# Diagonal matrices and FFN products moved from GpSimd to VectorE, and two more PSUM banks for a feed-forward stage

## The reference: what is computed

```python
xn = layernorm(x)                                   # over the features, eps 1e-5
# recurrent branch, D_INNER = 2048, 16 states per channel
x1, x2 = split(xn @ in_proj_w.T + in_proj_b)        # 2048 + 2048 features
u = silu(causal_conv4(x1) + conv_b)                 # depthwise, 4 taps
h[t] = dA * h[t-1] + dB * u[t];  y[t] = sum_n C[:, n] * h[t][:, n]
s = (y * silu(x2)) @ out_proj_w.T + out_proj_b
# feed-forward branch, HIDDEN = 3072, int weights / 127
g = silu((silu(xn @ wg.T) * (xn @ wu.T)) @ wd.T)
out = x + s * g
```

## Time and profile before

| | |
|---|---|
| median of 3 runs | 4397.6 us (4396.36 to 4398.45) |
| profiled execution, its own time | 4412.73 us |
| its span, slowest core (core 0) | 4411.2 us; the 8 cores 4382.3 to 4411.2 |
| PE busy | 2854.1 us (65%), mean granted clock 0.80 |
| DVE busy | 2549.1 us (58%), of which the 512 scans 2352.0 |
| POOL busy | 2634.7 us (60%), of which the 512 diagonals 1771.2 |
| ACT busy | 774.2 us (18%) |

### The profile page before, as it was taken

One profiled execution on the slowest core, in us unless ns is written; L12 is line 12 of the kernel. 1 busy time (PEld: TensorE's weight loads), 2 busy tenths in 40 slices (PEclk: granted clock), 3 DMA queues, 4 the chain that ended last, 5 costly groups with the idle time before them and its releaser, 6 DMA issues.

```text
span 4411.2 us, 32972 instructions; the slowest of 8 cores (4382.3 to 4411.2 us)
## 1 busy us (share of the span) xinstructions
PE 2854.1 (65%) x10752; PEld 1123.5 (25%) x10752; DVE 2549.1 (58%) x771; ACT 774.2 (18%) x1159; POOL 2634.7 (60%) x1060
## 2 busy tenths in 40 slices
PE   3666666666666567788636666666666665687976
PEld 1222222222222123233312222222222221233333
DVE  2888788887888811000138878888788888010001
ACT  6111111111111111231161111111111110112311
POOL 0788887888788820231008878888788888102310
PEclk9777777777777779899957777777777776897889
DMA  3010111101111053633320000110101000526333
GB/s 93 17 19 17 19 22 24 19 17 19 27 20 19 12 122 62 154 63 68 79 84 19 17 19 17 29 19 17 19 17 29 17 19 15 134 48 158 60 65 77
DMA packets 84542, 195.57 MB, mean 44 GB/s; under 512 B 10272, under 2 KB 27040, under 8 KB 84384
## 3 DMA queue, kind: packets, MB, share of 16 engines
q0 software_dynamic: 46080, 109.07, 15.1%
q1 hardware_dynamic: 38304, 84.40, 5.7%
HBM read 268.93 MB, written 33.55 MB: 69 GB/s over the span
## 4 chain that ended last, share of the span: by engine, by line
PE 37%; POOL 26%; issue 25%; DMA 6%; ACT 3%; DVE 2%; SPq 1%; POOLq 0%; DVEq 0%; ACTq 0%
POOL bfb L588 19%; PE ps_y L600 5%; POOL bfb L529 5%; PE ps_a L437 5%; PE ps_a L796 4%; PE ps_b L437 4%; PE ps_b L796 4%; PE ps_a L486 3%; PE ps_b L486 2%; PE ps_b L546 2%; PE ps_b L699 2%; PE ps_a L699 2%; POOL bfa L396 2%; PE ps_a L546 2%; DMA bfa<-wur 2%
## 5 line engine op out<-in xcount | busy, mean ns | idle before, releaser
L580 DVE TENSOR_TENSOR_SCAN bfb<-aa,bfb 128x2048 bf16<-128x2048 f32 x512 | 2352.0, 4654 | 451.5 <-PE ps_y L600 404.6
L588 POOL TENSOR_SCALAR bfb<-idbs,cbt 128x128 bf16<-128x128 bf16 x512 | 1771.2, 3468 | 307.7 <-PE ps_y L600 305.1
L600 PE MATMUL ps_y<-bfb 128*128 128x512 bf16 x2048 | 706.7, 488 | 920.9 <-POOL bfb L588 881.7
L739 DVE TENSOR_TENSOR bfb<-f32a,s_sb 128x1024 bf16<-128x1024 f32 x32 | 39.2, 1226 | 1108.8 <-ACT f32a L805 1108.8
L600 PEld LDWEIGHTS ps_y<-bfb 128*128 128x128 bf16 x2048 | 207.9, 112 | 1346.3 <-issue 1249.4
L437 PE MATMUL ps_a<-xnt,bfa 128*128 128x512 bf16 x1536 | 453.0, 448 | 85.8 <-DMA bfa<-wur 31.7
L529 POOL TENSOR_SCALAR bfb<-idbs,convws 128x128 bf16<-128x128 bf16 x128 | 310.6, 2440 | 176.4 <-DVE bfb L516 176.4
L396 POOL TENSOR_TENSOR bfa<-s_sb 128x1024 bf16<-128x1024 bf16 x96 | 381.5, 3974 | 11.8 <-ACT s_sb L450 11.1
L437 PE MATMUL ps_b<-xnt,bfa 128*128 128x512 bf16 x1536 | 385.9, 397 | 0.0
L486 PE MATMUL ps_a<-xnt,bfa 128*128 128x512 bf16 x1024 | 343.0, 495 | 4.2 <-ACT xnt L363 2.7
L450 ACT ACTIVATE s_sb<-ps_a,cnss 128x512 bf16<-128x512 f32 x192 | 131.9, 687 | 895.6 <-PE ps_a L437 894.2
(11 more groups left out here) (54 smaller groups left out, 1534.1 us busy)
## 6 DMA issues: line engine op xcount, KB each, us to landing
f32a<-x SPq DMA_DIRECT2D x64, 512.0 KB, 7.1
bfa<-wgr POOLq DMA_DIRECT2D x96, 256.0 KB, 3.7
bfa<-wur POOLq DMA_DIRECT2D x96, 256.0 KB, 3.6
bfb<-wdr POOLq DMA_DIRECT2D x32, 768.0 KB, 6.7
bfa<-winr POOLq DMA_DIRECT2D x64, 256.0 KB, 4.3
xg_spill<-bfb SPq DMA_DIRECT2D x32, 512.0 KB, 2.6
bfa<-woutr POOLq DMA_DIRECT2D x32, 512.0 KB, 5.2
bfb<-xg_spill SPq DMA_DIRECT2D x128, 128.0 KB, 5.2
```

Of the source, the lines that this page charges most:

```text
L580: (lambda i, n, hs, uslot: lambda e: e.tensor_tensor_scan(hs, sb["aa"][:, 16 * i + n:16 * i + n + 1].broadcast_to([128, T]), uslot, 0.0, A ...
L588: (lambda i, n, dg: lambda e: e.tensor_scalar_mul(dg, sb["idbs"][:], sb["cbt"][:, 16 * i + n:16 * i + n + 1]))(i, n, dg),
L600: (lambda n, pc, dg, hs: lambda e: e.matmul(ps["y"][:, 512 * pc:512 * (pc + 1)], dg, hs[:, 512 * pc:512 * (pc + 1)], start=(n == 0), stop= ...
```

## The change

Three kinds of work go from POOL's list to DVE's, at the same places of the order: the 128 tap diagonals of the convolution (L529), the 512 state diagonals `dg` (L588) and the 96 products `hm` (L396). They raise `sv` in place of `sg`, and who waited for `sg` waits for `sv`; `sg` goes. Diagonal n no longer waits for the matmuls of n-2 by itself: it stands right behind scan n in DVE's list, and that scan waits for them. The matmuls of n wait only for diagonal n, which comes after scan n. POOL is left with the weight loads.

The second part touches the stage of 48 feed-forward units at cb = 1: it gets a rotation of four banks, `ps["a"]`, `ps["b"]` and the first two banks of `ps["y"]`, which stand idle there. Before the next sequence's first matmuls into `ps["y"]`, PE waits for the last evacuations of those two (`psy_guard`).

```diff
         def flush_hm():
...
-                ev_hm[mh] = op("gpsimd",
+                ev_hm[mh] = op("vector",
...
-                               waits=wh, inc="sg")
+                               waits=wh, inc="sv")
...
-                    idx, fr = rot.acquire()
-                    psm = PSR[idx]
+                    idx, fr = f1_rot[0].acquire()
+                    psm = f1_rot[1][idx]
...
-                ev_cdiag[i] = op("gpsimd",
+                ev_cdiag[i] = op("vector",
...
-                ev_dg = op("gpsimd",
+                ev_dg = op("vector",
                            (lambda i, n, dg: lambda e: e.tensor_scalar_mul(
                                dg, sb["idbs"][:],
                                sb["cbt"][:, 16 * i + n:16 * i + n + 1]))(i, n, dg),
-                           waits=[("st", ev_hfree)], inc="sg")
+                           inc="sv")
...
-                        w = [("sg", ev_dg), ("sv", ev_scan[(i, n)])]
+                        w = [("sv", ev_dg)]
                         if n == 0:
                             w.append(("sv", ev_gate.get(i - 1, 0)))
+                        if n == 0 and i == 0 and 0 in psy_guard:
+                            w.append(psy_guard.pop(0))
+                            w.append(psy_guard.pop(1))
...
+                rot_f1 = RotN(4)
+                rot_f1.free[0] = rot.free[0]
+                rot_f1.free[1] = rot.free[1]
+                rot_f1.free[2] = ("sv", ev_b_end_v)
+                rot_f1.free[3] = ("sv", ev_b_end_v)
+                f1_rot[0] = rot_f1
+                f1_rot[1] = (PSR[0], PSR[1],
+                             ps["y"][:, 0:512], ps["y"][:, 512:1024])
...
+                rot.free[0] = rot_f1.free[0]
+                rot.free[1] = rot_f1.free[1]
+                psy_guard[0] = rot_f1.free[2]
+                psy_guard[1] = rot_f1.free[3]
+                f1_rot[0] = rot
+                f1_rot[1] = PSR
```

More of the change, by code:

```diff
@@ L35 @@
 ENGS = ("sync", "gpsimd", "vector", "scalar", "tensor")
-SEMS = ("sg", "q0", "qx0", "qx1", "qx2", "qx3", "qxg", "qxg2", "qxp", "qs",
+SEMS = ("q0", "qx0", "qx1", "qx2", "qx3", "qxg", "qxg2", "qxp", "qs",
         "qsx0",
@@ L274, in build_schedule @@
     SX2_SLOT = (bfb[:, 8192:10240], bfb[:, 14336:16384])
+    psy_guard = {}
     for u in range(BPC):
@@ L387, in build_schedule @@
         f1_last_mm = [0]
+        f1_rot = [rot, PSR]
         pending_hm = []
@@ L431, in emit_f1_mms @@
                             if p == 0 and hi == 0:
-                                w.append(("sg", ev_hm[mh - 2] if mh >= 2
+                                w.append(("sv", ev_hm[mh - 2] if mh >= 2
                                           else ev_hm_prev[0]))
@@ L453, in emit_f1_mms @@
                                                  waits=wev, inc="ss")
-                    rot.release(idx, "ss", ev_mm_evac[(mh, hi, p)])
+                    f1_rot[0].release(idx, "ss", ev_mm_evac[(mh, hi, p)])
                 if mh == 1 and hi == 1:
@@ L532, in emit_conv @@
                                      sb["convws"][:, 4 * i + kk:4 * i + kk + 1]))(i, kk),
-                                 waits=w, inc="sg")
+                                 waits=w, inc="sv")
             uslot = bfb[:, 4096 + 2048 * (i % 2):4096 + 2048 * (i % 2) + 2048]
@@ L542, in emit_conv @@
                     if kk == 0:
-                        w = [fr, ("sg", ev_cdiag[i]),
+                        w = [fr, ("sv", ev_cdiag[i]),
                              ("ss", ev_x1evac[(i, p)])]
@@ L713, in build_schedule @@
                                           waits=[("st", lastm),
-                                                 ("sg", ev_f1_all_hm)], inc="ss")
+                                                 ("sv", ev_f1_all_hm)], inc="ss")
                     rot.release(idx, "ss", ev_sevac[(m, p)])
@@ L793, in build_schedule @@
                                 w.append(("sv", ev_g_done_v))
-                                w.append(("sg", ev_hm_prev[0]))
+                                w.append(("sv", ev_hm_prev[0]))
                         lastm = op("tensor",
```

## The result

The median of the changed kernel's 10 runs is 3980.4 us against 4403.7 us for 10 of the kernel before; the ratio of undisturbed runs is 0.9042, 95% interval 0.903 to 0.9053, so 9.6% faster. The prediction said 4052 us, within 3965 to 4165: right in direction and range, 72 us too little gain.

The account below looks back on a forecast made before the run. Scans on DVE were taken to wait for PE and PE for POOL. Savings of 322 us in the scan stage, 18 at the output projection and 6 from banks, 346 off 4412.7, gave 4052 us after run adjustment, range 3965 to 4165.

Parts of the forecast that it names:

- The bound and its loop: Scan stage, 1457 us a sequence: no engine full; scans wait for PE's matmuls, PE for POOL's diagonals (411 us) and taps.
- Scans at 4.34: Scan stage on DVE: with POOL idle each scan takes 4.34 us start to start, 69.4 us for 16 a group.
- Small instructions at 0.20: State and tap diagonals on DVE: 0.20 us each in series, bounds 0.10 and 0.33; 20 a group, 4.0 us.
- Products at 1.0: Products on DVE in the scan stage: 1.0 us each, three in two groups, 1.5 us a group.
- Gate at 5.1: DVE's gate ending each group: 2.3 us plus an unchanged 2.8 us wait for the last matmuls, 5.1 us.
- PE's chains at 1.2: Scans' waits behind PE's runs of 28 matmuls after n = 1 and n = 9: 1.2 us a group for both.
- Output projection at cb = 1: Its first weights load earlier, ending PE's stand and slow first matmuls: 9 us gained each sequence, 18 in all.
- Four banks: Feed-forward units at cb = 1: evacuation waits mostly become weight waits; 3 us gained each sequence, 6 in all, bounds 0 and 22.
- Rivals: Alternatives: PE at lower clock 11%, small instructions at 0.33 us 8%, scans at 4.52 us 5%, slower 4%, no effect 2%.
- the 0.74 at which it would have turned the sign: Slower-than-before rival, 4%: a small instruction behind a scan on DVE at 0.74 us would eat the whole 346 us.
- The middle case of the first rival: Scan stage: 20 of 28 chain matmuls at the lower clock, waits 2.3 and 1.5 us, 78 us back, 4130 us.
- the first rival: Scan stage: PE becomes the bound, its 28-matmul chains wholly at lower clock, 270 us back, 4320 us; 11% in part or whole.

Follow-up runs that it names:

- The two halves tried alone: Kernel before with only the state diagonals moved to DVE: ratio 0.9203; changed kernel with the state diagonals back on POOL: ratio 0.9102.
- the second experiment: Changed kernel with the 512 state diagonals and their wait back on POOL, taps and products on DVE, four banks: 4013.2 and 4016.3 us, ratio 0.9102.
- the fourth experiment: Changed kernel with cb = 1 products on POOL and the first cb = 0 output-projection weights held until the scan stage's last matmuls: 4009.2 and 4009.5 us.

## Why the prediction was right, and where it was off

- **The bound and its loop** (scans wait for PE, PE for POOL): right, with one correction. The prediction took the diagonals as what PE waited for, by the 411 us of the earlier trace rows. The two halves tried alone gain 339 and 383 us of 420, so no part owns the gain. Shown is that each alone takes away nearly all of the scans' wait, and that the 411 us are no measure of it: with the diagonals left on POOL most of them stay (296 us in 1100) and the gain is there. That the places of taps and products in POOL's list made the scans late is read from the timeline.
- **Scans at 4.34** from the two with POOL idle: right; 4.33 in the changed kernel, all 512 between 4.41 and 4.43 as records.
- **Small instructions at 0.20**: too high; 0.15 in series (0.16 for taps), 2.9 us a group instead of 4.0. The record, 0.233, is within the bound of 0.29, but the next instruction starts 0.09 before its end, and the price by column taken from a float32 row overstated a bf16 instruction: 35 us of the difference.
- **Products at 1.0**: too high; 0.60 in series, 0.9 a group instead of 1.5. The record is 0.689. The estimate from the Trainium skill ("VectorE: DVE Perf Modes", section "The perf-mode tier table") was 0.7; by that rule double rate applies when all is bf16, and the trace agrees. 19 us.
- **Gate at 5.1**: 2.2 + 2.3 = 4.5. The wait was 2.77 since POOL's diagonal of n = 15 ended after its scan (931.60 against 931.19 us in the timeline ahead of the first gate of the earlier trace rows); I let it stay; with the diagonals on POOL again (the second experiment) it is 2.77 again. 19 us.
- **PE's chains at 1.2**: 1.2, though not in the shares of the prediction, which had 0.4 us behind n = 1 and 0.5 behind the convolution. Of the 18.1 us in 15 groups 15.0 stand behind the convolution, in every group, and 3.0 behind n = 1, in three of them.
- These are the mis-sized terms of the sum: 78.9 instead of 81.2 us a group, 32 times, 73 us. 1260.5 and 1255.7 us for the stage instead of 1295. That 73 is so near the 72 us by which the forecast was off is chance. From span to span the sum had 346 us and 431.2 were measured, 85 more: 73 in the stage, 12 at cb = 0, 8 at cb = 1, and 9 lost elsewhere. The medians show less of it, since the profiled execution of the kernel before lay 15.1 us above its median and that of the changed one 1.1 above.
- **Output projection at cb = 1**: the mechanism is shown by the fourth experiment; the gain of 9 for each sequence fits the 8.6 us wait there. **The join at cb = 0** was missed: the prediction looked at who waits for the weight loads there and found nobody, and not at what they delay, the store that they run beside. 12 us.
- **Four banks**: 6 predicted; the 5 us between the medians can't be told from that or from nothing, and most of the wait reappears as a wait for weights, as said. The second sequence's stretch at cb = 1 got 20.7 us shorter, which join and banks don't cover; most of the rest is the lower clock that cores 0 and 1 had there in that one execution of the kernel before, 0.82 for this core.
- **Rivals.** None came in. The granted clock of the scan stage rose from 0.76 to 0.81 instead of staying low; the price of a small instruction is a fifth of the 0.74 at which it would have turned the sign. The middle case of the first rival, 20 of 28 matmuls at the lower level, is added up wrong there: with its own prices the two waits are 2.6 and 2.8 us, not 2.3 and 1.5, which makes about 4175 us instead of 4130, above the range.

## What to carry to other kernels

When an engine in a loop is slow because another holds it up, ask who waits for it before asking how busy it is: POOL at 91% beside the scans cost 37 us, while with products and taps between those same diagonals, and the joins that hang on them, it cost 420. The total of a wait is no price either, if the engine that waits is not the bound. A short instruction is priced by the distance of the starts around it, not by its record. And a load that is issued earlier can shorten a later transfer that would have run beside it, so both sides of a join are to be read.

## What the runs showed of the hardware that was not expected

- DVE and POOL hold each other up for whole instructions in both directions: a 128x128 instruction on POOL takes 0.60 us alone and 4.0 to 4.5 us beside scans, and a 0.23 us one on DVE took 2.04 us behind a product on POOL. What DVE loses to a short one on POOL is only 0.07 us; a scan that meets a product there was up to 6.28 us long instead of 4.42.
- ACT makes the same diagonal in 0.394 us on average beside the scans, with none over 0.402, so it isn't held.
- Four matmuls of 512 columns ahead of the gate took 1.87 us where PE's last unit of 16 was three steps earlier and 1.02 where it was two (granted clock 0.50 and 1.00); the place of filler work in this loop sets the clock of the work behind it.
